# Adapter scales one block later, LoRA load behind the weight loads, last table chunk behind the first group's splits

## What is computed

```python
x = x + einsum('bct,bcd->bdt', x, W0[ids0])              # L0: a 64x64 matrix chosen by row
x = x + (conv(x, K1) + x * D1) * (t < len1)              # L1: causal convolution over t, a kernel for each channel
x = x + x @ W.T + bias + s[a] * ((x @ A[a].T) @ B[a].T)  # L2: dense over t (1024x1024), with a LoRA adapter a for each row
x = x + (conv(x * m, K3) + x * m * D3) * m               # L3: causal convolution, m = (t < len3)
# K = 2 * einsum('hn,hnl->hl', Ct, exp(dt*A * l)).real, 64 complex modes for each of 64 channels, length 1024
# adapters: 8, rank 16; s: 8 scaling factors
```

## Time and profile before

| | us |
|---|---|
| median of 3 runs | 1727.7 (1726.52 to 1729.54) |
| the profiled execution | 1726.97, span 1725.2 |
| PE busy | 1582.3 (92%) |
| DVE busy | 1042.2 (60%) |
| POOL busy | 812.2 (47%) |
| ACT busy | 531.0 (31%) |

### The profile page before, as it was taken

The page is one execution under the profiler, slowest core; times in us unless marked ns, Lnnn a source line. Parts: engine busy times, 40 slices in busy tenths (PEclk is TensorE's granted clock), DMA queues, the critical chain, the costliest instruction groups (busy, mean ns, idle before and its releaser), DMA issues.

```text
span 1725.2 us, 31102 instructions
## 1 busy us (share of the span) xinstructions
PE 1582.3 (92%) x12183; PEld 1036.6 (60%) x12183; DVE 1042.2 (60%) x1328; ACT 531.0 (31%) x674; POOL 812.2 (47%) x365
## 2 busy tenths in 40 slices
PE   6577773799999999999999999999999999999996
PEld 6576762457474747474747474747474747474744
DVE  7576766456666666566666666665656565656532
ACT  4334342223232323232323232323232323232311
POOL 2000003325656564747474747474738383838334
PEclk9788886899999999999999999999999999999999
DMA  5799995125362525252525252525253535343314
GB/s 132 188 324 340 333 357 181 49 56 150 54 152 52 149 47 152 49 151 53 143 61 139 66 139 66 139 66 130 74 126 78 126 78 125 79 115 84 78 49 98
DMA packets 405475, 216.81 MB, mean 126 GB/s; under 512 B 223480, under 2 KB 391936, under 8 KB 402368
## 3 DMA queue, kind: packets, MB, share of 16 engines
q1 hardware_dynamic: 386112, 204.20, 44.5%
q10 hardware_dynamic: 19328, 12.14, 2.6%
HBM read 94.19 MB, written 71.76 MB: 96 GB/s over the span
## 4 chain that ended last, share of the span: by engine, by line
PE 80%; DVE 7%; DMA 4%; issue 3%; SPq 3%; ACT 1%; ACTq 0%; POOL 0%; DVEq 0%; POOLq 0%
PE ps L728 38%; PE ps L763 7%; PE ps L666 7%; PE ps L693 6%; PE ps L720 5%; PE ps L736 5%; DMA arena<-in_x_dram 4%; PE ps L776 3%; PE ps L670 3%; PE ps L710 2%; PE ps L610 2%; SPq L354 1%; SPq L347 1%; PE ps L706 1%; PE ps L561 1%
## 5 line engine op out<-in xcount | busy, mean ns | idle before, releaser
L728 PE MATMUL ps<-arena,w2t 128*128 128x512 f16 x3072 | 681.3, 379 | 0.0
L728 PEld LDWEIGHTS ps<-arena,w2t 128*128 128x128 f16 x3072 | 300.6, 98 | 362.4
L529 POOL TENSOR_TENSOR arena<-arena 128x1024 f32<-128x1024 f16 x64 | 143.7, 2246 | 548.6 <-DMA arena<-arena 530.9
L1464 DVE TENSOR_SCALAR arena<-ps,biasx 128x512 f32<-128x512 f32 x128 | 94.6, 750 | 244.9 <-ACT arena L1054 244.2
L1054 ACT ACTIVATE arena<-ps,biasx 128x512 f16<-128x512 f32 x128 | 87.2, 688 | 447.9 <-PE ps L736 447.9
L505 POOL TENSOR_TENSOR arena<-arena 128x1024 f32<-128x1024 f32 x32 | 76.3, 2385 | 312.5 <-DMA arena<-tab_scratch 275.7
L610 PE MATMUL ps<-arena 128*128 128x128 f32 x1024 | 150.6, 310 | 65.6 <-DMA arena<-in_x_dram 42.4
L610 PEld LDWEIGHTS ps<-arena 128*128 128x128 f32 x1024 | 140.6, 220 | 73.4 <-DMA arena<-in_x_dram 48.2
L693 PE MATMUL ps<-arena 128*128 128x512 f16 (+1 forms) x768 | 137.3, 329 | 7.8 <-DVE arena L1385 6.6
L763 PE MATMUL ps<-arena 128*128 128x256 f16 (+1 forms) x1536 | 138.5, 247 | 3.2 <-DVE arena L1458 3.0
L532 POOL TENSOR_TENSOR arena<-arena,one_xs 128x1024 f32<-128x1024 f32 x64 | 136.6, 2135 | 5.0
(11 more groups left out here) (211 smaller groups left out, 2109.9 us busy)
## 6 DMA issues: line engine op xcount, KB each, us to landing
arena<-in_x_dram SPq DMA_DIRECT2D x128, 256.0 KB, 7.0
out_dram<-arena SPq DMA_DIRECT2D x64, 512.0 KB, 3.1
gbuf<-x_scratch SPq DMA_DIRECT2D x120, 256.0 KB, 3.2
x_scratch<-arena SPq DMA_DIRECT2D x24, 1024.0 KB, 8.5
arena<-krow_scratch SPq DMA_DIRECT2D x32, 512.0 KB, 4.2
arena<-tab_scratch SPq DMA_DIRECT2D x32, 200.0 KB, 2.6
x_scratch<-arena SPq DMA_DIRECT2D x8, 768.0 KB, 7.1
gbuf<-in_L_cond_weight_dram ACTq DMA_DIRECT2D x8, 512.0 KB, 6.8
```

The costliest lines, as they stand in the source:

```text
L529: nc.gpsimd.tensor_tensor(past[:, h % 2].rearrange("p (k t) -> p k t", k=NBLK), x3t[:, h % 2, 0], x3t[:, h % 2, 1], ALU.add).then_inc(past ...
L728: nc.tensor.matmul(ps[:, 4 + o % 3, :], w2t[:, part, k, o * P:(o + 1) * P], xx[:, :, k, :], start=(k == 0 and q == 0), stop=False)
```

## The change

Four things are moved, and two access patterns are changed:
- **Adapter scales.** Three of the four operations of `adapter_scales` go to the parameters at the very start (two make the adapter number of each partition, one the mask in `adapter_scale`); one multiplication by the loaded scale is left, and it stands, with the wait for the eight loads, in step 4 of the second block.
- **LoRA load.** The order of the lots is now A, W0, W1, B, W2 and so on: in the first block's step 6 only the weight block W1 is loaded; LoRA B is loaded in step 0 of the second block, into the other row buffer, turned in step 6, and its low part made after the second block. `lot_target` and `turned_tiles` for LoRA B are written so that the result is contiguous and the PSUM source strided, the other way round than before.
- **Order within a block.** `combine_b` moves from step 7 to step 0 of the next block, behind the last odd copy; `store_tab` from step 0 to step 1; `lot_hi` from 7 to 6; `lot_lo` from step 1 of the next block to 7. The stores of a block stand at pieces 6, 7, 8, 9.
- **Transition.** `combine_b` of the last chunk comes after `table_lo(0, 0)`; `store_tab` of it after the states; `scale_k`, `split_k` and `store_k` after the second splits; `sum_k` after the last far product. `turn_u(0, 0)` stands ahead of the stores of the last block, and SP's wait for the earlier stores of `x1_stored[0]` is dropped there.

```diff
--- before.py
+++ after.py
@@ -282,25 +282,26 @@
         ssm = (ssm1, ssm3)
         NLINK = 19
 
-        LOT_A, LOT_W0, LOT_B, LOT_W = 0, 1, 2, 2
+        LOT_A, LOT_W0, LOT_W1, LOT_B, LOT_W = 0, 1, 2, 3, 2
 
         x_pairs = x.rearrange("(n q) c t -> (q c) n t", q=2)
 
         def weight_block(n):
 
-            return 0 if isinstance(n, int) and n == LOT_W0 else n - LOT_W
+            return n - LOT_W0 if isinstance(n, int) and n in (LOT_W0, LOT_W1) else n - LOT_W
 
         def lot_target(n, part):
 
             if isinstance(n, int) and n == LOT_B:
-                return bt[:, part, :].rearrange("p (o j) -> p j o", j=NBLK)
+                return bt[:, part, :].rearrange("p (o j) -> p o j", j=NBLK)
             if isinstance(n, int) and n == LOT_A:
                 return at[:, part, :, :]
             return w2t[:, part, :, bass.ds(weight_block(n) * P, P)]
 
         def turned_tiles(n):
 
-            return ps[:, 6:8, :].rearrange("p q (m o) -> p (q m) o", m=4)
+            tiles = ps[:, 6:8, :].rearrange("p q (m o) -> p (q m) o", m=4)
+            return tiles.rearrange("p m o -> p o m") if isinstance(n, int) and n == LOT_B else tiles
 
         def row_of(n, parity):
 
@@ -355,7 +356,7 @@
                              xq[:, k, d0:d1].rearrange("p d b -> p (d b)")).then_inc(x1_stored[k][part], 16)
 
 
-            STORE_AT = {6: 0, 8: 1, 10: 2, 12: 3}
+            STORE_AT = {6: 0, 7: 1, 8: 2, 9: 3}
 
             def stage0(i, first):
                 for m in range(2 * STEPS):
@@ -395,12 +396,10 @@
             sp.wait_ge(s0_summed, NBLK * STEPS)
             sp.wait_ge(krow_stored, 16 + 32)
             load_g(0, 0)
+            wait_u(0, 0)
+            turn_u(0, 0)
             for part in range(NPART):
                 store_x1(NBLK // 2 - 1, 1, part)
-            for part in range(NPART):
-                sp.wait_ge(x1_stored[0][part], 16 * NBLK // 2)
-            wait_u(0, 0)
-            turn_u(0, 0)
             sp.wait_ge(krow_stored, 16 + 32 * NBLK)
             for r in range(2):
                 sp.wait_ge(tab_stored[r], 16 * NBLK // 2)
@@ -586,7 +585,7 @@
             def turn_lot(n, parity=None):
 
                 if isinstance(n, int) and n in (LOT_A, LOT_B):
-                    pe.wait_ge(wrow_loaded[0], 16 * (1 + n // 2))
+                    pe.wait_ge(wrow_loaded[n % 2], 16 * (1 + n // 2))
                 else:
                     pe.wait_ge(w2_ready, weight_block(n) + 1)
                 at_least(pe, w2_hi, n)
@@ -623,17 +622,16 @@
                         if step == 1:
                             sum_k(blk - 1)
                         if first and step == 3:
+                            turn_lot(LOT_W1)
+                        if first and step == 6:
                             turn_lot(LOT_B)
-                        if step == 5:
+                        if not first and step == 5:
                             turn_lot(blk + LOT_W, k)
 
             pe.wait_ge(iota_done, 5)
             stage0(0, True)
             with pe.Fori(1, NBLK // 2) as i:
                 stage0(i, False)
-            sum_k(NBLK - 1)
-
-
             pe.wait_ge(s0_even_out, NBLK * STEPS // 2)
             pe.wait_ge(s0_odd_out, NBLK * STEPS // 2)
 
@@ -795,6 +793,7 @@
                 if h >= 2:
                     near1(0, h)
                 far1(0, h)
+            sum_k(NBLK - 1)
             pe.wait_ge(k_scaled, NBLK)
 
             def body(g, more1):
@@ -843,8 +842,8 @@
                 if not (isinstance(n, int) and n == LOT_W0):
                     act.wait_ge(w2_turned, n - 1)
                 if isinstance(n, int) and n == LOT_B:
-                    act.dma_start(wrow[0].rearrange("p (m a r) -> p m a r", m=NBLK, a=NADAPT),
-                                  lora_b.rearrange("a (p m) r -> p m a r", m=NBLK)).then_inc(wrow_loaded[0], 16)
+                    act.dma_start(wrow[1].rearrange("p (m a r) -> p m a r", m=NBLK, a=NADAPT),
+                                  lora_b.rearrange("a (p m) r -> p m a r", m=NBLK)).then_inc(wrow_loaded[1], 16)
                 else:
                     act.dma_start(row_of(n, parity), w2[bass.ds(weight_block(n) * P, P), :]).then_inc(
                         wrow_loaded[n % 2 if parity is None else parity], 16)
@@ -957,20 +956,24 @@
                             lot_hi(LOT_A)
                         if step == 6:
                             lot_hi(LOT_W0)
-                            load_lot(LOT_B)
-                            load_lot(LOT_W + 1, 0, 1)
+                            load_lot(LOT_W1)
                     else:
-                        if step == 0:
+                        if step == 1:
                             store_tab(blk - 1, 1 - k)
-                            if not (first and k == 1):
-                                load_lot(blk + LOT_W, i, k)
                         if step == 2:
                             scale_k(blk - 1)
+                        if first and step == 0:
+                            load_lot(LOT_B)
                         if first and step == 4:
+                            lot_hi(LOT_W1)
+                        if first and step == 7:
                             lot_hi(LOT_B)
+                        if not first and step == 0:
+                            load_lot(blk + LOT_W, i, k)
+                        if not first and step == 6:
+                            lot_hi(blk + LOT_W)
                         if step == 7:
                             store_k(blk - 1)
-                            lot_hi(blk + LOT_W)
                     chunk_sines(blk, k, step)
 
             stage0(0, True)
@@ -1031,15 +1034,15 @@
             for h in range(HG):
                 x1_split_hi(0, h)
             bases_hi(0, 0)
-            store_tab(NBLK - 1, 1)
-            scale_k(NBLK - 1)
             table_hi(0, 0)
-            store_k(NBLK - 1)
             act.wait_ge(tab_stored[0], 16 * NBLK // 2)
             for k in range(NCH - 1):
                 state_hi(0, 0, k)
+            store_tab(NBLK - 1, 1)
             for h in range(HG):
                 x2_split_hi(0, h)
+            scale_k(NBLK - 1)
+            store_k(NBLK - 1)
             for h in range(HG):
                 x1_split_hi(1, h)
             act.wait_ge(tab_stored[1], 16 * NBLK // 2)
@@ -1166,6 +1169,9 @@
             link(nc.vector.reciprocal(t[7], t[4]))
 
 
+            link(ts(rank_adapter, pcol, 1.0 / RANK, -0.5 + 0.5 / RANK, ALU.mult, ALU.add))
+            link(ts(rank_adapter, rank_adapter, ROUND, ROUND, ALU.add, ALU.subtract))
+            ts(adapter_scale[:, :], idf[:, 2, :], rank_adapter, None, ALU.is_equal)
             link(ts(quarter_own, pcol, float(C), 0.25, ALU.is_lt, ALU.mult))
             link(ts(quarter_adv, quarter_own, 0.25, None, ALU.add))
             for n, (half, quarter) in enumerate(((half_own, quarter_own), (half_adv, quarter_adv))):
@@ -1238,10 +1244,7 @@
             def adapter_scales():
 
                 dve.wait_ge(consts_loaded, 16 * NADAPT)
-                link(ts(rank_adapter, pcol, 1.0 / RANK, -0.5 + 0.5 / RANK, ALU.mult, ALU.add))
-                link(ts(rank_adapter, rank_adapter, ROUND, ROUND, ALU.add, ALU.subtract))
-                link(ts(rank_scale, rank_scale, XS / FS, None, ALU.mult))
-                ts(adapter_scale[:, :], idf[:, 2, :], rank_adapter, rank_scale, ALU.is_equal, ALU.mult)
+                ts(adapter_scale[:, :], adapter_scale[:, :], rank_scale, XS / FS, ALU.mult, ALU.mult)
 
             def right_angles(c, r, i):
                 at_least(dve, tab_stored[r], 16 * i)
@@ -1294,8 +1297,8 @@
 
             def lot_ready(n, i, parity):
 
-                if isinstance(n, int) and n == LOT_W0:
-                    dve.wait_ge(wrow_loaded[1], 16)
+                if isinstance(n, int):
+                    dve.wait_ge(wrow_loaded[parity], 16 * (1 + n // 2))
                 else:
                     dve.wait_ge(wrow_loaded[parity], 16 * (i + 2))
                 own = wrow[parity][:, bass.ds(weight_block(n) * P, P)]
@@ -1348,16 +1351,21 @@
                             lot_ready(LOT_W0, 0, 1)
                         if step == 5:
                             lot_lo(LOT_A)
-                            adapter_scales()
                         if step == 7:
                             lot_lo(LOT_W0)
                     else:
-                        if step == 1 and not (first and blk == 1):
-                            lot_lo(blk - 1 + LOT_W)
+                        if step == 0:
+                            combine_b(blk - 1, 1 - k)
+                        if first and step == 2:
+                            lot_ready(LOT_W1, 0, 0)
+                        if first and step == 4:
+                            adapter_scales()
                         if first and step == 5:
-                            lot_lo(LOT_B)
-                        if step == 4:
+                            lot_lo(LOT_W1)
+                        if not first and step == 4:
```

(10 more changed lines are left out.)

## The result

| | before | changed |
|---|---|---|
| median of 6 runs each, us | 1728.16 (1726.52 to 1730.15) | 1720.81 (1717.65 to 1722.89) |
| profiled execution, us | 1726.97, span 1725.2 | 1718.66, span 1716.9 |
| first store of block 0 starts at | 71.88 | 55.13 |
| store of block 1 starts at | 100.03 | 88.55 |
| last matmul of stage 0 ends at | 264.04 | 261.67 |

The ratio is 0.9954 [0.9941, 0.9966]: faster by 7.4 us, where 17.2 were forecast. 1720.8 is also above the stated range (1698 to 1719). The forecast in the same three parts was -12.3, -7.9 and +3.0; measured: **-2.4, -13.9 and +8.0**. The errors of the three (+9.9, -6.0, +5.0) partly cancel, so the whole error is 8.9, less than that of stage 0 alone.

A forecast was written before the change was run, and what follows sets the result against it. It took stage 0 as bound by DMA transfers and the groups by PE. Stage 0 12.3 + transition 7.9 - late group 1 3.0 = 17.2 us off 1726.97 gave 1709.8, as median 1710.5; range 1698 to 1719.

The forecast's parts named there:

- the same three parts: Stage 0, the transition to group 0's dense stage, and the rest: forecast -12.3, -7.9 and +3.0 us.
- Part 1, adapter scales: Stage 0, ahead of 72 us: the 13.44 us stall goes and the first store leaves earlier; gain 10.0, bounds 5 and 11.
- The LoRA block: Second block: the LoRA load keeps ACT's queue about 8 us, covered; as a rival, uncovered, 1716 us, chance 0.14.
- The named cover: Stage 0: four stores and loads up to 29, already issued, keep DMA engines busy beyond 72 us; without it, up to 5.
- Part 2, packed stores: Stores at pieces 6 to 9 in stage 0: packing changes nothing if reads and stores are one stream of work.
- the rival that said otherwise: Stage 0: loads resume only after four packed stores, so each of seven blocks grows; 1733 us at 3.3 each, chance 0.05.
- The other half of part 2: Block borders in stage 0: `combine_b` behind the last odd copy gains 0.4 us each, 2.3 in all, between 0 and 6.
- SP's border wait: SP's wait at the 6 block borders inside the loop, 3.1 us each, taken as mostly bridged by the DMA engines.
- Part 3, transition: After stage 0: splits beside POOL, near products 4.7 us earlier, states 7.0 earlier; with POOL's earlier start 7.9 in all.
- the chain (29.6 us): The stretch from the states to group 0's dense stage, forecast to stay the same length.
- Part 4, group 1 late: Group 0's dense stage: late loads make PE stop 3 us, between 0 and 8; as rival 1718 us, chance 0.14.
- proof against itself: The prediction is wrong if PE waits over 8 us in group 0's dense stage.

The follow-up runs named there:

- spread stores: Changed kernel with the stores of a block at pieces 6, 8, 10, 12 again: 1703.42 us, ratio 0.9839.
- the kernel of 1693.5: Changed kernel with stores at pieces 6, 8, 10, 12 and SP loading group 1, then the tables, before its krow wait: 1693.5 us, ratio 0.9797.
- SP's order: Changed kernel with SP loading the two tables and group 1 ahead of its wait for the last kernel rows: 1716.55 us, ratio 0.9911.

## Why the prediction was wrong, step by step

**Part 1, adapter scales: right.** "Gain: 72 - 62 = 10.0": alone it measures 10.6 by the medians, while in its profile stage 0 ends 7.2 earlier, inside the stated bounds of 5 and 11. The three operations at the start cost nothing: DVE's copy at 36.46 starts to the hundredth where it did before.

**The LoRA block: right that it is covered, wrong in its length.** "The LoRA load keeps ACT's queue for about 8 us again": 14.43 here, 16.71 with spread stores, 11.99 in the kernel of 1693.5. The named cover held: with PE at nothing from 62 to 74 us the DMA share is 1.11 at 359 GB/s. Removing the stop brought 2.1, within the scatter of the runs, and the two ways to schedule around it brought nothing or cost 3 to 4.

**Part 2, packed stores: the step that failed.** "If reads and stores are one stream of work, packing changes nothing" went into the sum as 0, and the rival that said otherwise got 0.05. It costs 17 in the changed kernel and 16 in the one before (20 and 15 by the ratios). That rival's own numbers were good: it named 2.5 us for each block as the point from which the change loses, and the interval of 28.8 against 26.3 is just that. What was wrong is the argument against it, DVE's busy time of 132.5 of 190.3 us: a mean over the stage, where the question was whether eight slots bridge four stores in a row. They don't, and it hits twice. While the stores move, PE starves and its clock falls; then a long row of loads (13 in 19.22 us) is issued at the pace at which PE frees slots, and the DMA engines idle. That this is how the time is lost is read from the windows and waits; what is shown by removing and adding it is the price of the order. A share of 1.06 was taken as a bound that only depends on the bytes. Its mean fell to 1.00 with the gaps that packing leaves, and at almost the same share (1.07) the spread stores moved 357 GB/s instead of 335. What sets the rate at a given share was not isolated.

Here the Trainium skill ("Trainium Kernel Development and Optimization", Key Constraints) says that DMAs issued from the queues of SP, ACT and POOL run on the same 16 engines and interleave. The trace agrees that they stay shared and full: while the stores of block 1 move and PE gets few pieces, the share is 1.07 and 1.04 (96 to 104 us). But the rule is about several queues; the loads and stores of x stand in one, SP's, and these runs show that their order in it is worth 1%. That transfers interleave does not mean that their order is free.

The other half of part 2 was mis-sized the other way: `combine_b` behind the last odd copy shortens the interval by 1.7 us for each block instead of 0.4. The 3.1 us of SP's border wait were counted as bridged by what was queued; by the intervals, about half of them were not. Stage 0, forecast 12.3 earlier, is 17.3 earlier with spread stores (264.04 to 246.78) and 2.4 with packed ones. Of the 17.3 the scales alone show 7.2 and `combine_b`'s place 3.8. The 6.2 between the kernel with the scales alone (stage 0 to 256.81) and the one with everything but packed stores and `combine_b`'s new place (250.60) come from the other moves, the LoRA lot among them, which the prediction put at 0; no run separates them. All three are single profiles: kernels with the same program up to there end stage 0 at 243.68, 245.60 and 246.78.

**Part 3, transition: direction right, size and reason wrong.** Forecast 7.9, measured 13.9. The changed kernel, with POOL among its rows:

```profile
257.08 2.23 POOL L504 TENSOR_TENSOR arena<-arena 128x1024 f32<-128x1024 f32 x1 [247.05 <-DMA arena<-tab_scratch]
257.44 2.15 DVE L1269 TENSOR_TENSOR arena<-arena,gbuf 128x256 f32<-128x256 f32 x1
271.71 4.63 DVE L1422 SCALAR_TENSOR_TENSOR arena<-gbuf,arena 128x1024 f16<-128x1024 f32 x4 [1.19 <-ACT arena L989]
277.15 6.51 PE L691 MATMUL ps<-arena 128*128 128x512 f16 x24 [15.48 <-DVE arena L1391]
283.50 1.50 PE L664 MATMUL ps<-arena 128*128 128x128 f16 x24
309.50 7.00 PE L718 MATMUL ps<-arena,at 128*128 128x512 f16 x24 [5.55 <-DVE arena L1434]
```

I had the four splits beside POOL, the last of them done 14.3 and the near products at 17.3 behind the last matmul. Here POOL started 6.3 us earlier than before and so ran against `combine_a` of the last block (L1269, 2.15 instead of 0.42), and the splits were free (4.63). With spread stores and in the kernel of 1693.5 POOL does meet the splits; they take 10.69 and 11.11 and the near products start 16.4 and 16.7 behind the last matmul: the forecast said 17.3. So the mechanism and its price held, and which operations pay it moves with the timing of a store. The Trainium skill ("SBUF — State Buffer", Who interferes with whom) says that who issues first decides who blocks. The trace agrees: L1269 takes 0.42 without POOL beside it (at 242.26 with spread stores) and 2.15 where it starts 0.36 behind POOL's L504, which takes 2.23.

The larger error is behind the states. "From the states to the dense stage the chain (29.6 us) is the same": it took 26.0 (283.50 to 309.50). The windows show two differences. Before, in 300 to 310 us, the granted clock was 0.62 and POOL was busy 9.55 of the 10 us; in the changed kernel, in 287 to 297, the clock was 1.00 and POOL did nothing, since its tables were done. The rows tell them apart. One state's six matmuls, before and in the changed kernel:

```profile
300.29 0.85 PE L666 MATMUL ps<-arena 128*128 128x128 f16 x6
287.02 0.50 PE L664 MATMUL ps<-arena 128*128 128x128 f16 x6
```

PE's waits for ACT between the states are the same in both (1.52 and 1.46). From the first state to DVE's first second split it is 17.3 before (296.16 to 313.41) and 13.9 in the changed kernel (283.50 to 297.44): so 3.3 of the 3.6 us lie in matmuls at the lower clock, and the remaining 0.3 in one second split beside POOL (1.54 against 1.23). The same 26.0 stands with spread stores (269.75 to 295.74) and in the kernel of 1693.5 (266.16 to 292.15). The prediction's 29.6 held half-clock matmuls that it took for a fixed part of the chain.

**Part 4, group 1 late: right place, a third of the size.** Forecast +3.0 (0 to 8), measured +8.0 in the last part.

```profile
312.31 0.39 SPq L374 DMA_DIRECT2D arena<-krow_scratch  x1
313.98 6.70 SPq L382 DMA_DIRECT2D gbuf<-x_scratch  x8
318.13 1.93 POOL L504 TENSOR_TENSOR arena<-arena 128x1024 f32<-128x1024 f32 x1 [46.70 <-DMA arena<-tab_scratch]
320.96 11.09 DVE L1422 SCALAR_TENSOR_TENSOR arena<-gbuf,arena 128x1024 f16<-128x1024 f32 x4 [10.76 <-ACT arena L989]
334.94 2.72 PE L734 MATMUL ps<-gbuf,bt 128*128 128x512 f16 x6 [8.08 <-DVE gbuf L1457]
```

```profile
332.00:340.00 8.00, 5.06 (x12) 1.76 (x13) 4.37 (x7) 2.95 (x4) 5.63 (x3) 0.50 0.00 0
```

PE waits 8.08 where 3 was forecast, just above the 8 that the prediction named as proof against itself. The loads came nearly as worked out (issued from 313.98; the last high split ends at 327.42, 1.0 later than the forecast's terms give). The term that failed is one low split of "1.2 to 2.9" behind the last part: DVE makes all four, POOL's tables start 2.8 us before them, and the four need 11.09. I had priced the last one and left out the queue of the three ahead of it. Behind the wait the clock is 0.50 until 340: six products take 2.72 instead of 1.46, and the 24 weight matmuls behind them 6.70 (from 337.45) instead of 5.34 before, together 2.6 more. The LoRA A sums ahead of the wait had been 1.1 faster (7.00 against 8.11), so that the third product, at 343.99, stands 34.5 behind the dense start against 24.8 before: 9.7, the wait and a net 1.6. Some 1.7 of it come back later, and I have not followed where. SP's order undoes all of it (1399.2 and 1397.6 in the last part).

**The sum with measured sizes:** 17.3 for stage 0, less 14.9 for packing, 13.9 for the transition, less 8.0 for part 4: 8.3, the difference of the two spans.

## What to carry to other kernels

Where loads and large stores share one queue and the loads feed a few slots, interleave them: four stores of 0.75 to 1 MB with one load between each cost 16 to 17 us here (15 to 20 by the ratios), and one store at every second load was enough. Judge such a step not by busy shares of the stage but by whether the slots last through the longest run of stores, and count the clock that the starved engine loses. And when a wait is moved to the front of a queue, price everything that is freed at once behind it with its neighbours running, not the last item alone. Loads that need nothing can stand ahead of it, unless they set off an engine that holds a busy one: with the tables ahead the transition gave back 4.5 us, with the tables last it did not.

## What the runs showed of the hardware

- An issue on ACT's queue behind one load of 8192 pieces of 64 B sat 11.99 to 16.71 us in the kernels with the first store near 55 us, and ACT's own work with it; behind 1024 pieces of 512 B it took 0.49. In four kernels whose ACT program has the LoRA load elsewhere, or whose first store goes out later, it is 7.98 (before), 8.21 (packed stores alone), 8.58 (scales alone) and 3.97 (`combine_b` in step 7): the length is no property of the load alone. What sets it was not isolated.
- The same load landed 28.6 us after its issue when it was issued 6 us later among the stores (58.47 to 87.04).
- DVE and POOL operations that exclude each other slow both engines: four splits take 4.63 alone and 6.36 to 11.11 beside POOL, by how many of them meet it, and POOL's L510 takes 2.79 beside them against 1.93 when they are done.
- A wait of 8 us in the groups, where PE is otherwise busy 99% of the time, is followed by matmuls at half clock that take 2.6 us longer (9.42 against 6.80 us for the same 30).
- The DMA share is no measure of the rate: 1.06 at 335 GB/s in the kernel before, 1.07 at 357 with the stores of the changed kernel spread (stage 0, 90 to 230 us and 90 to 220 us).
